# Scores of self-attention from two 32-bit pieces, two heads above each other, with the stacks and shift rows loaded through Pool's queue

## The reference

```
q = (x @ wq).reshape(B, T, H, D)            # H = 16 heads, D = 16, T = 2048
lat = x @ w_down
k = (lat @ wk_up).reshape(B, T, H, D)
v = (lat @ wv_up).reshape(B, T, H, D)
q = _apply_rope(q, cos, sin)
k = _apply_rope(k, cos, sin)
scores = jnp.einsum('bqhd,bkhd->bhqk', q, k) * scale
allowed = pages[None, :] <= pages[:, None]  # pages of 64 tokens
scores = jnp.where(allowed[None, None], scores, jnp.finfo(scores.dtype).min)
attn = jax.nn.softmax(scores, axis=-1)
out = jnp.einsum('bhqk,bkhd->bqhd', attn, v).reshape(B, T, E)
```

## Time and profile before

| | us |
|---|---|
| time before, median of 2 runs | 871.35 (870.32 to 872.37) |
| the profiled execution, its time | 868.17 |
| its span, first to last instruction | 866.4 |

### The profile page before, as it was taken

One profiled execution on the slowest core, in us unless ns is written; L12 is line 12 of the kernel. 1 busy time (PEld: TensorE's weight loads), 2 busy tenths in 40 slices (PEclk: granted clock), 3 DMA queues, 4 the chain that ended last, 5 costly groups with the idle time before them and its releaser, 6 DMA issues. The chain is left out here.

```text
span 866.4 us, 11677 instructions
## 1 busy us (share of the span) xinstructions
PE 791.3 (91%) x4137; PEld 389.8 (45%) x4137; DVE 577.3 (67%) x1049; ACT 411.0 (47%) x843; POOL 156.3 (18%) x218
## 2 busy tenths in 40 slices
PE   8874887999899999989999979998799999999967
PEld 6441222333232332223333312885467667767756
DVE  5999578889988899978887610376125456446524
ACT  1551453776477766557777769121322222222231
POOL 2662000000000000000000000132305544544530
PEclk9985799999999999989999989999999999999988
DMA  7795311200000000000630000200111122122002
GB/s 208 219 259 160 98 51 37 62 26 25 2 1 2 2 1 2 1 1 1 194 90 1 2 1 1 107 1 0 38 39 52 63 76 76 38 76 76 0 1 97
DMA packets 27087, 47.31 MB, mean 55 GB/s; under 512 B 6048, under 2 KB 22944, under 8 KB 26272
## 3 DMA queue, kind: packets, MB, share of 16 engines
q1 hardware_dynamic: 24096, 43.81, 16.8%
q10 hardware_dynamic: 2944, 2.89, 1.2%
HBM read 38.16 MB, written 8.39 MB: 54 GB/s over the span
## 5 line engine op out<-in xcount | busy, mean ns | idle before, releaser
L477 DVE TENSOR_REDUCE part_max<-psum 128x1 f32<-128x512 f32 (+3 forms) x560 | 342.4, 669 | 64.7 <-PE psum L676 59.3
L589 ACT ACTIVATE probs<-psum 128x512 f32<-128x512 f32 (+3 forms) x640 | 293.7, 541 | 164.9 <-PE psum L701 152.4
L676 PE MATMUL psum<-k_stack,q_stack 96*128 96x512 bf16 (+4 forms) x640 | 216.4, 366 | 18.7 <-DVE psum L463 11.2
L701 PE MATMUL psum<-q_stack,k_stack 98*128 98x512 bf16 (+4 forms) x640 | 205.4, 360 | 18.6 <-DMA q_stack<-shift 13.0
L713 PE MATMUL psum<-probs,v_all 128*17 128x512 f32 (+3 forms) x1280 | 149.9, 541 | 0.3 <-PE psum L687 0.2
L676 PEld LDWEIGHTS psum<-k_stack,q_stack 96*128 96x128 bf16 (+1 forms) x640 | 60.4, 99 | 172.5 <-DVE part_max L477 119.9
L701 PEld LDWEIGHTS psum<-q_stack,k_stack 98*128 98x128 bf16 (+1 forms) x640 | 61.5, 100 | 102.6 <-ACT probs L589 46.0
L1356 PE MATMUL psum<-q_stack,qc_t 128*128 128x512 f32 (+1 forms) x256 | 91.5, 510 | 2.6 <-ACT qc_t L1332 2.1
L1383 PE MATMUL psum<-v_out,p_t 128*128 128x256 f32 (+1 forms) x416 | 92.7, 380 | 0.0
L878 POOL MEMSET eps<- 128x4 f32 x1 | 0.1, 101 | 470.1 <-POOLq L272 470.1
L1383 PEld LDWEIGHTS psum<-v_out,p_t 128*128 128x128 f32 (+1 forms) x416 | 77.8, 190 | 9.9
(11 more groups left out here) (130 smaller groups left out, 645.8 us busy)
## 6 DMA issues: line engine op xcount, KB each, us to landing
mask<-in_mask SPq DMA_DIRECT2D x16, 800.5 KB, 4.3
pieces<-k_stack SPq DMA_DIRECT2D x24, 256.0 KB, 4.8
q_stack<-pieces SPq DMA_DIRECT2D x24, 256.0 KB, 4.3
k_stack<-pieces SPq DMA_DIRECT2D x24, 256.0 KB, 4.7
x_sb<-in_x SPq DMA_DIRECT2D x4, 512.0 KB, 9.3
out<-y SPq DMA_DIRECT2D x4, 512.0 KB, 2.8
q_stack<-in_ctxT SPq DMA_DIRECT2D x1, 1601.0 KB, 10.0
probs<-in_cos ACTq DMA_DIRECT2D x4, 256.0 KB
```

Source lines behind the costliest of these rows:

```text
L477: nc.vector.tensor_reduce(part_max[:, h:h + m, r, c:c + 1], src, axis=AX_X, op=ALU.max).then_inc(m_read, 1)
L589: nc.scalar.activation(probs[:, s % 2, h, col:BLK], s_bank[h][:, col:BLK], ACT.Exp, scale=ATTN_SCALE).then_inc(exp_done, 1)
L676: last = nc.tensor.matmul(out, q_stack[b][0:rows, g * G + h, r * P:(r + 1) * P], k_stack[c][0:rows, g * G + h, 0:keys], start=True, stop=True)
L701: nc.tensor.matmul(s_bank[h][:, col:BLK], k_stack[s // TPB][0:rows, g * G + h, (s % TPB) * P:(s % TPB + 1) * P], q_stack[b][0:rows, g * G ...
```

## The change

1. q and k are cut into two pieces instead of three, each a float32r number (a matmul of this type takes one pass). Products: three instead of six, 48 rows a head, with two shift and four mask rows 54.
2. Two heads lie above each other: a stack holds head pairs, one on partitions 0 to 53, the other on 64 to 117 (`PAR`, `ROOM`), with 8 slots of 512 32-bit columns where 16 slots of bf16 were. Each matmul of scores or maxima reads one of the halves; consecutive scores alternate between halves, and units do so in the opposite order.
3. The third piece and its work are gone (L380, L438, half of ACT's cuts). Pieces in HBM are 32 bits wide: 16 sends of 512 KB in place of 24 of 256 KB. Stack loads stay 12 of 256 KB a block; the extra rows take 16 transfers of 96 KB in place of 8.
4. Stack loads, extra rows and shift rows are issued by Pool, in Pool's instruction stream; SP keeps the sends, x and the prefetch.
5. The split of `neg_max` in two parts moves ahead of the turn: two small VectorE operations on 128 partitions, then one copy of 32 turned rows behind it.
6. Units of the diagonal block hold two heads at most: a group has 12, 28, 44 or 60 units in place of 11, 27, 43 or 59, with the same columns in all.

```diff
-Q_PIECES = [0, 0, 0, 1, 1, 2]
-K_PIECES = [0, 1, 2, 0, 1, 0]
+Q_PIECES = [0, 0, 1]
+K_PIECES = [0, 1, 0]
+PIECES = 2
+PAR = 2
+HP = H // PAR
+ROOM = P // PAR
...
-    units = [[(h, r, c, BLK, 0)] for c in range(b) for r in range(TPB) for h in range(G)]
+    heads = [(par, n) for n in range(G // PAR) for par in reversed(range(PAR))]
+    units = [[(par, n, r, c, BLK, 0)] for c in range(b) for r in range(TPB) for par, n in heads]
     for r in range(TPB):
         keys = P * (r + 1)
-        per = BLK // keys
-        per = per if G % per == 0 else 1
-        units += [[(h + n, r, b, keys, n * keys) for n in range(per)] for h in range(0, G, per)]
+        if G // PAR * keys <= BLK:
+            units += [[(par, n, r, b, keys, n * keys) for n in range(G // PAR)] for par in reversed(range(PAR))]
+        else:
+            units += [[(par, n, r, b, keys, 0)] for par, n in heads]
...
+            for b in range(2):
+                load_extra_rows(nc.gpsimd, io, q_stack[b], k_stack[b], extra_loaded[b])
             for tb in range(NB):
                 rotate(tb)
-                last_piece(tb)
                 if tb == 0:
                     norm(3)
+                if tb:
+                    for n in range(PIECES):
+                        if tb < NB - 1:
+                            load(tb - 1, n)
+
+            pool.wait_ge(prod_done, 8 * NB)
+            pool.wait_ge(v_ready, 2 * NB)
+            for n in range(PIECES):
+                for r in range(2):
+                    pool.wait_ge(piece_sent[n][r], 16 * NB)
+            for b in range(2, NB):
+                load_extra_rows(nc.gpsimd, io, q_stack[b], k_stack[b], extra_loaded[b])
+            late = [(b, n, (s,)) for b in range(2, NB) for n in range(PIECES) for s in range(2)]
+            for k, (b, g) in enumerate(order):
+                send_shift(b, g)
+                if k < 2 * NG:
+
+                    pool.wait_ge(shift_sent, 16 * PAR * (k + 1))
+                    for into, n, which in late[len(late) * k // (2 * NG):len(late) * (k + 1) // (2 * NG)]:
+                        load(into, n, which)
...
+                            dve.wait_ge(neg_max_done, index(b, g) + 1)
+                            whole_max = neg_max[:, :].rearrange("p (v q) -> p v q", v=PAR)
+                            nc.vector.tensor_copy(neg_parts[:, :, 0, :], whole_max).then_inc(neg_parts_done, 1)
+                            dve.wait_ge(neg_parts_done, index(b, g) * 2 + 1)
+                            nc.vector.tensor_tensor(neg_parts[:, :, 1, :], whole_max,
+                                                    neg_parts[:, :, 0, :].bitcast(F32), ALU.subtract)\
+                                .then_inc(neg_parts_done, 1)
...
-                for s in range(1, steps[b]):
-                    if s == steps[b] - 2 and not late:
-                        send_shift(*following(b, g))
-                    step(b, g, s)
-                if following(b, g):
-                    if late:
-                        send_shift(*following(b, g))
...
-                rows = STACK if s >= TPB * b else SHIFTED
+                rows = slice(h % PAR * ROOM, h % PAR * ROOM + (STACK if s >= TPB * b else SHIFTED))
+                at = g * (G // PAR) + h // PAR
```

218 lines of the change are left out of this document (89 added, 129 removed).

## The result

The changed kernel takes 921.68 us (921.59 to 921.78, two runs) against 871.35 of before: ratio 1.058, interval 1.052 to 1.063. It is slower by 50 us; I had forecast 850, with 828 to 884 as range. The profiled execution has a span of 919.9 us. Executions of one kernel here can lie a few per cent apart, the slower ones at a lower granted clock, so the ratios here compare the faster ones and medians of few runs carry up to 10 us of doubt.

What follows compares the result with a forecast made beforehand. Attention was taken as a race between PE, ahead in a block's first groups, and VectorE, in its last. Attention -26.8, start +5 and last chain +1 gave -20.8 us, so 850 us from 871.35, range 828 to 884.

Steps and rivals of the forecast that it cites:

- first scores: Start of attention: first scores at some 94 to 96 us in place of 88.86, taken as +5 us.
- block 1: Attention block 1, paced by VectorE with its waits for shift rows gone: 87.5 us against 92.70, -5.2.
- block 2: Attention block 2, paced by VectorE with its waits for shift rows gone: 130.7 us against 139.70, -9.0.
- group 14, with the last chain: Group 14, ACT next to pace: 40 us, -5; the last chain's wait for shift rows gets 1 us longer.
- Two of the signs: Wrong if VectorE under 92% with PE free, PE waits for stack loads, or clock slices under 0.9 between 150 and 500 us.
- I take pairs: Scores and units run two at once, 0.228 us a pair; PE's load in group 13 falls from 40.6 to 28.6 us.
- none are paired: Scores and units in group 13 without any pairing: 26.4 us in place of 25, 1.3 us more than now.
- VectorE at 96.5%: VectorE paces blocks 1 and 2 and groups 12 and 13, busy for 96.5%: 87.5, 130.7 and 77.8 us.
- The clock: Rival, chance 0.12: PE with too little work drops to 1.2 GHz; 897 to 932 us, taken as 905.
- the trace before shows the clock fall only behind stops: Argument against the clock rival: in the earlier trace the clock fell behind stops and came back in 5 to 6 us.
- I leave equal: Block 0's groups, led by the shift chain: Pool's rows land later but ACT is no longer blocked; change 0.
- Pool's queue: Pool issues loads and shift rows at 1.0 us each in the preparation; start +5 us, range +3 to +20.

Runs made afterwards that it cites:

- e4: Changed kernel with phases of back-to-back 32-bit matmuls ahead (alternate halves, one half, 102 rows); 1118 us, 249 us of it phases ahead.
- e1: Changed kernel, late extra rows issued behind the first shift rows, every score and maxima matmul over rows 0 to 117, so none run side by side; 916.4 us.
- e14: Changed kernel with score and maxima matmuls reading the upper 16 bits of each operand as bf16, all else the same; 872.1 us.
- e13: Kernel before, bf16 pieces and own queues, with scores and maxima using only half the rows so two can run side by side; 863.7 us.
- e6: Changed kernel with phases ahead in which PE waits for a VectorE reduction, then issues one, two or four matmuls per beat; 1330 us.
- e15: Changed kernel with first shift rows issued ahead of Pool's wait for the sends, extra rows of blocks 2 and 3 behind them; 915.9 us.
- e8: Kernel before with only its shift rows issued by Pool's queue in place of ACT's; 858.8 us, ratio 0.983.

## Why the prediction was wrong

The terms of the sum by the profiled spans, in us against the kernel before:

| term | forecast | measured |
|---|---|---|
| first scores | +5 | +6.7 |
| block 0 behind them | 0 | +11.6 |
| block 1 | -5.2 | +15.1 |
| block 2 | -9.0 | +19.7 |
| groups 12 and 13 | -7.6 | +1.8 |
| group 14, with the last chain | -5 and +1 | -1.1 |
| group 15 | 0 | +1.8 |
| behind attention | 0 | -2.1 |
| sum | -20.8 | +53.5 |

Two of the signs by which the prediction said it would be wrong came: VectorE is busy for 78% of blocks 1 and 2 and 85% of groups 12 and 13, and slices between 150 and 500 us stand at a clock of 0.5.

*TensorE's part, "I take pairs": right in form, wrong in what it is worth.* Units and scores do start in twos, 0.24 us apart once PE runs, and 400 back to back cost 0.23 a couple (e4). But the price came from a warm-up that never stops, where the next load is done ahead. In the real order couples are single, behind a wait, and then the load is paid: 0.34 us. The same step failed for "none are paired", 1.3 us more in group 13: 4.0 (e1). With bf16 operands the couple behind a stop costs 0.24 us (e14).

*Who is late next, "VectorE at 96.5%": failed for the 32-bit type, held for bf16.* Groups 12 and 13, forecast 77.8 us, took 87.2; group 13, at a clock of 1.00, took 41.8 for the forecast 38.9, with VectorE at 89%. With bf16 halves it is 38.4 and 39.1 us (e13, e14), against my 38.9.

*The clock: this rival came true, and I gave it 0.12.* It said 897 to 932, and 921.7 came; but its arithmetic missed, and the range was met in part by luck. It put the low share at 0.7 to 0.8 and said that VectorE hides it up to 0.53; the shares were 0.50 and 0.46 in blocks 1 and 2, and yet these were 20.3 and 28.7 us over the forecast. One reason is that low stretches come in one piece: nearly all of group 11 lay in one, and its 13.9 us can't be hidden by groups that run at 1.00. The other is the price of the couples, which it didn't have. Its formula gives 28.6/0.52 = 55 us for a group like 13 at group 11's clock of 0.52; group 11 has fewer matmuls (215 in the row, against 257) and took 56.4, so the formula is too low there too. The argument that I set against it failed: at the low level PE is not busy without a pause, since scores, exponentials and reductions still wait on one another, and a low stretch is not over in 5 to 6 us. I had read "the trace before shows the clock fall only behind stops" as a rule; the likely reading, by e6, is that the kernel before has no steady stretch with so little for PE to do. The Trainium skill (TensorE: Matmul & The Clock Gate, A second HAM failure mode) was the better guide: e6 shows a clock that falls on pauses of about half a microsecond (0.72 less the 0.23 of a couple), with no long one among them.

*Block 0, "I leave equal": failed.* It was given nothing and cost 11.6 us, at a clock of 0.50 to 0.56. With bf16 operands it takes 61.3 us from first scores to end in place of 70.2 (e14), so most of this is the type with the clock as well.

*Pool's queue.* Issues cost 0.57 us, less than the 1.0 I took; preparation ended sooner (shift rows written at 80.9 us, before at about 84). First scores at 95.5 lie in my 94 to 96, and the start's +5 was +7, but that is luck in the parts: I had the sends done at 84, 8 us of issues and 1.8 us to landing; it was 81.9, 4.5 and 8.4 to 8.6. The shift rows landed so late because eight loads stood ahead of them, the order that I had listed myself (e15). That shift rows in Pool's queue take away the wait of 2.79 us at 376 and the clock's fall behind it is right (e8), and worth 8 us by the spans and 16 by the medians, not 5.

*Group 14, last chain, group 15.* 44.3 for the forecast 40 (41.0 with bf16). The last chain's wait for shift rows is 3.13 us, before 3.68, so its +1 didn't come; group 15, left equal, took 32.6 for 30.8.

The account of 71.7 us from my 850 to 921.7: 49.6 are the type with the clock that it holds down (e14), and 22.1 are left. By e14's stages 6.8 of these stand at the end of block 0 (159.2 for the forecast 152.4), and 6.5, 5.3, 3.4 and 1.0 behind it (94.0, 136.0, 81.2 and 41.0 against 87.5, 130.7, 77.8 and 40), at clocks of 0.89 to 0.96; these parts are by one trace and add up to 23.0. How the 49.6 part into direct pace and clock no run isolates: groups 9 and 13 give 6% of direct price, which on e14's 431 us from the first output copy to the last is an estimate of 27 us, and the clock some 23. It takes for granted that groups at the low clock and those that VectorE paces pay the same 6%, which no run shows.

## What to carry to other kernels

Work taken from TensorE is worth nothing where another engine paces, and can cost: PE that rested for more than half of each beat lost its clock in e6 and in group 11, and everything it did then, the value matmuls that weren't touched too, took nearly twice as long (1.91 us for 1.05). Before halving PE's work, ask at what share of the pace it will stream, and price the low level, not only the gain. Take the price of a couple or a load from a place with the same waits around it; a warm-up shows only the back-to-back one. When a load is moved in a queue, look at what now stands behind it: here the wait went from the first group to the second. And part a change: here its small piece, shift rows in a queue of their own, was worth 1.7% alone, and the large one cost 5.8% with it.
